# A lone half block as the sixteenth single block, row numbers read ahead, and turnings and the last shared batch in another order

## What is computed

```python
x = L0_attn_x                                  # 8 x 256 tokens, 256 features
x = x + attention(layernorm(x))                # 16 heads, running sums of phi(k) * v
h = layernorm(x)
logits = h @ router_w                          # 8 experts
top_logits, top_indices = top_k(logits, 2)
scores = softmax(top_logits)
routed: for each token and each of its 2 experts e
    g, u = split(h @ w1[e]); y = (silu(g) * u) @ w2[e]; out += score * y     # 256 -> 2*512 -> 256
shared = (silu(h @ w_gate) * (h @ w_up)) @ w_down                            # 256 -> 1024 -> 256
out = x + routed + shared
```

## Time and profile before

| what | value |
|---|---|
| median of 3 runs | 350.57 us (350.32 to 350.61) |
| the profiled execution, its own time | 352.41 us |
| its span, first to last instruction | 350.8 us |
| TensorE busy | 336.1 us, 96% of the span |
| VectorE / ScalarE / GpSimd busy | 235.2 / 203.8 / 199.8 us |
| mean granted TensorE clock | 0.997 |

### The profile page before, as it was taken

One profiled execution on the slowest core, in us unless ns is written; L12 is line 12 of the kernel. 1 busy time (PEld: TensorE's weight loads), 2 busy tenths in 40 slices (PEclk: granted clock), 3 DMA queues, 4 the chain that ended last, 5 costly groups with the idle time before them and its releaser, 6 DMA issues.

```text
span 350.8 us, 9452 instructions
## 1 busy us (share of the span) xinstructions
PE 336.1 (96%) x3082; PEld 276.6 (79%) x3082; DVE 235.2 (67%) x584; ACT 203.8 (58%) x369; POOL 199.8 (57%) x299
## 2 busy tenths in 40 slices
PE   8999999999999999999999999999899999999991
PEld 7779878888888888988988455656468888888880
DVE  4999989899889887878788565555433344443440
ACT  2779959797887987746536354364353434443340
POOL 4776567786875868565656443453443453336443
PEclk9999999999999999999999999999999999999998
DMA  7992152564965556735774345667674176544434
GB/s 190 390 348 49 30 127 48 131 150 160 198 198 91 150 164 144 214 102 132 256 260 110 96 68 74 101 88 86 97 103 68 22 95 73 62 63 61 62 44 48
DMA packets 65774, 43.43 MB, mean 124 GB/s; under 512 B 49600, under 2 KB 60864, under 8 KB 65344
## 3 DMA queue, kind: packets, MB, share of 16 engines
q1 hardware_dynamic: 51664, 32.32, 36.0%
q0 software_dynamic: 9392, 10.44, 18.8%
q10 hardware_dynamic: 4672, 0.07, 1.0%
HBM read 19.09 MB, written 12.97 MB: 91 GB/s over the span
## 4 chain that ended last, share of the span: by engine, by line
PE 69%; DVE 14%; issue 5%; DMA 5%; ACT 3%; SPq 2%; POOL 0%; POOLq 0%; DVEq 0%
PE bU L247 13%; PE bG L247 13%; PE bU L1153 6%; PE bD L1030 5%; PE bG L1153 5%; PE bV L1218 4%; PE bQ L1218 3%; DVE ab L1694 3%; PE bQ L1174 3%; PE bV L1174 3%; PE bQ L247 2%; PE bV L247 2%; DMA xT<-rows 2%; PE bK L247 2%; DMA wd<-in_w_att 2%
## 5 line engine op out<-in xcount | busy, mean ns | idle before, releaser
L1694 DVE SCALAR_TENSOR_TENSOR ab<-bU,sg 128x512 f32<-128x512 f32 x64 | 44.2, 690 | 65.3 <-PE bU L247 32.1
L825 POOL DMA_INDIRECT out_y<-xs,dst_row x32 | 50.0, 1563 | 57.7 <-DVE dst_row L2037 28.1
L1343 ACT ACTIVATE sg<-bG 128x512 f32<-128x512 f32 x64 | 38.0, 593 | 45.4 <-PE bG L247 26.1
L598 POOL DMA_INDIRECT x_rows<-rows,slot_u x32 | 42.2, 1318 | 15.3 <-issue 14.2
L1508 ACT ACTIVATE ws_h<-ab 128x512 f16<-128x512 f32 x36 | 22.7, 629 | 47.0 <-DVE ab L1694 43.0
L2022 DVE TENSOR_TENSOR ws_h<-ab,ws_h 128x512 f16<-128x512 f32 x36 | 25.0, 694 | 20.8 <-ACT ws_h L1508 19.7
L1350 ACT ACTIVATE ah<-ab 128x512 f16<-128x512 f32 x32 | 20.1, 629 | 28.9 <-DVE ab L1694 28.8
L247 PE MATMUL bG<-work,we 128*128 128x256 f16 x240 | 29.5, 273 | 0.0
L247 PE MATMUL bU<-work,we 128*128 128x256 f16 x240 | 29.5, 273 | 0.0
L247 PEld LDWEIGHTS bG<-work,we 128*128 x240 | 23.4, 98 | 2.9 <-issue 0.2
L247 PEld LDWEIGHTS bU<-work,we 128*128 x240 | 23.4, 98 | 2.7
(11 more groups left out here) (358 smaller groups left out, 874.0 us busy)
## 6 DMA issues: line engine op xcount, KB each, us to landing
stage<-in_w_expert SPq DMA_DIRECT2D x24, 512.0 KB
we<-in_w_shared SPq DMA_DIRECT2D x3, 1024.0 KB, 11.5
out_y<-xs SPq DMA_DIRECT2D x8, 256.0 KB
xs<-bo POOLq DMA_DIRECT2D x7, 256.0 KB, 4.3
xs<-in_x SPq DMA_DIRECT2D x1, 1280.0 KB, 17.5
x_rows<-we SPq DMA_DIRECT2D x9, 134.0 KB
xs<-in_x SPq DMA_DIRECT2D x3, 256.0 KB, 4.4
work<-x_rows SPq DMA_TRANSPOSE x40
```

What stands on the lines that cost most here:

```text
L598: pool.indirect_dma_start(xrows, bass.IndirectOffsetOnAxis(ap=slot_u[q][:, k, t:t + 1], axis=0), rows2[q][:, t, :].bitcast(U16), None).the ...
L825: pool.indirect_dma_start(out_rows, bass.IndirectOffsetOnAxis(ap=dst_row[:, b:b + 1], axis=0), ya[b % NY], None, bounds_check=NT * P - 1, ...
L1343: act.activation(sg[q][:], src[:], ACT.Silu, scale=1.0 / WS).then_inc(S["sg_done"], 1)
L1694: dve.scalar_tensor_tensor(out=ab[q][:], in0=src[:], scalar=1.0 / WS, in1=sg[q][:], op0=ALU.mult, op1=ALU.mult).then_inc(S["a_done"], 1)
```

## The change

1. Block 15 (`LONE`) becomes a half block of 64 rows. Gate and up are done in two column tiles: the same 64 rows are stationary in both, tile 0 makes columns 0 to 255 and tile 1 columns 256 to 511, so 6 pairs of matmuls of 256 columns. Its down is 12 pairs of 128 columns. The activations are 128 x 256 instead of 128 x 512, two matmuls turn them. Its weights come from the lent copies: four copies at the end of block 13 on VectorE and two at the end of block 15. Its meta data is loaded in two halves on ScalarE, its output goes out as half rows of 128 columns with one more small index operation on VectorE. GpSimd makes six more constants, four of them in the last group, `slot_constants(4)`.
2. SyncE reads 12 row numbers into registers of their own (upper halves of the four mixed blocks, blocks 4 to 11) after it has saved the last batch and before `turn_low(0)`; `load_rows` for these reads none.
3. `turn_high(b-1)` stands behind both up-projections of block b instead of between them, for b = 1, 2, the mixed blocks and 15.
4. In the last shared batch on VectorE `shared_out(6)` and the two spread copies move back, behind `swiglu` and `act_lo` of chunks 2 and 3; `expert_lo` of part 22 comes before them.

```diff
+    LONE = NS - 1
+    HALVED = MIXED + [LONE]
-    N_CONST = 41
+    N_CONST = 47
...
+        def width(b):
+            return FE // 2 if b == LONE else FE
...
+            ahead = [(b, 1) for b in MIXED] + [(b, 0) for b in range(NX, NX + 8)]
+            ahead_reg = {s: sp.alloc_register(f"row_of{s[0]}_{s[1]}") for s in ahead}
...
-                sp.reg_load(row_reg[t], blk_row[slot:slot + 1, :])
+                if (b, t) not in ahead:
+                    sp.reg_load(reg, blk_row[slot:slot + 1, :])
...
             save(B - 1)
+            for s in ahead:
+                slot = slot_of(*s)
+                sp.reg_load(ahead_reg[s], blk_row[slot:slot + 1, :])
...
+                elif b == LONE:
+                    pool.nop(nofuse=True)
+                    pool.indirect_dma_start(half_rows, bass.IndirectOffsetOnAxis(ap=dst_row[:, NBLK:NBLK + 1], axis=0),
+                                            ya[b % NY][:, 0:D // 2], None, bounds_check=2 * NT * P - 1, oob_is_err=False,
+                                            compute_op=ALU.add).then_inc(S[f"scattered{b % 2}"], 16)
...
+            def turned_late(b):
+                return b in HALVED or b in (1, 2)
...
+            def lone_up(half):
+                dst, done, free = ((bG, "g_ps", "sg_done"), (bU, "u_ps", "a_done"))[half]
+                if half == 0:
+                    pe.wait_ge(*rows_in(LONE))
+                    pe.wait_ge(S["lent"], 6 * NPAIR + 4)
+                pe.wait_ge(S[free], NP * B + LONE)
+                x2, n = xg[LONE % NX], FE // 2
+                for s, (hi, lo) in enumerate(((0, 0), (1, 0), (0, 1))):
+                    w = lent_up[:, lo, :].rearrange("p (k h n) -> p k h n", k=KC, h=2)
+                    for k in range(KC):
+                        for t in range(2):
+                            ins = pe.matmul(dst[t * HALF:(t + 1) * HALF, 0:n], x2[:, hi * KC + k, 0:HALF], w[:, k, half, t * n:(t + 1) * n],
+                                            start=s == 0 and k == 0, stop=s == 2 and k == KC - 1, skip_group_check=True)
...
+            def lone_down():
...
+                    for c in range(FC):
+                        at = c // 2 * HALF
+                        for t in range(2):
+                            ins = pe.matmul(dst[t * HALF:(t + 1) * HALF, 0:m], a[:, c % 2, at:at + HALF], lent_down[:, c, lo, t * m:(t + 1) * m],
...
             for b in range(NS):
-                expert_up(b, 0)
-                if b >= 1:
+                if b == LONE:
+                    lone_up(0)
+                    lone_up(1)
+                else:
+                    expert_up(b, 0)
+                    if b >= 1 and not turned_late(b):
+                        turn_high(b - 1)
+                    expert_up(b, 1)
+                if turned_late(b):
                     turn_high(b - 1)
-                expert_up(b, 1)
...
-                if b <= NS + 1:
+                if b == NS:
                     expert_down(b - 2)
+                elif b == NS + 1:
+                    lone_down()
...
-                parts = 2 if b in MIXED else 1
+                parts = 2 if b in HALVED else 1
...
             expert_lo(part_of_step(B, 4))
-            shared_out(B - 2)
             swiglu(n + 2, 0)
+            expert_lo(part_of_step(B, 5))
+            act_lo(j, 2)
+            swiglu(n + 3, 1, bV)
+            act_lo(j, 3)
             dve.wait_ge(S["spread_ps"], 1)
...
-            expert_lo(part_of_step(B, 5))
-            swiglu(n + 3, 1, bV)
-            act_lo(j, 2)
-            act_lo(j, 3)
             expert_lo(part_of_step(B, 6))
+            shared_out(B - 2)
...
+                if b == MIXED[-1]:
+                    for k in range(4):
+                        lend_weights(NPAIR, k)
+                if b == LONE:
+                    for k in range(4, 6):
+                        lend_weights(NPAIR, k)
```

More of the change, by code:

```diff
@@ L319, in meta_in @@
                 return S[f"first_meta{b}"], 16
-            return S[f"meta_in{b % NX}"], sum(32 if n in MIXED else 16 for n in range(b % NX + NX, b + 1, NX))
+            return S[f"meta_in{b % NX}"], sum(32 if n in HALVED else 16 for n in range(b % NX + NX, b + 1, NX))
         def paired(b):
@@ L338, in slot_of @@
         def slot_of(b, t):
-            return b if t == 0 else HALF + MIXED.index(b)
+            return b if t == 0 else HALF + HALVED.index(b)
+        def width(b):
+            return FE // 2 if b == LONE else FE
         def mixed_of(a):
@@ L607, in const @@
                     pool.wait_ge(S["slot_const"], n_const[0])
-            evens, list_pos, here = half_f[:, 1:NPAIR + 1], slot_w[:, 1, 0:1], slot_w[:, 0, 1:NPAIR + 1]
+            odds, list_pos, here, lone = half_f[:, 1:NPAIR + 1], slot_w[:, 1, 0:1], slot_w[:, 0, 1:NPAIR + 1], slot_w[:, 0, 0:1]
             def slot_constants(k):
@@ L643, in slot_constants @@
                     const(pool.tensor_scalar(pick_block[:], iota_f[:, 0:NBLK], place_at[:], None, ALU.is_equal))
-                    const(pool.tensor_scalar(slot_w[:, 2, 0:1], upper[:, 1:2], 1.0, None, ALU.mult), wait=True)
+                    const(pool.tensor_scalar(lone, place_at[:], float(LONE), None, ALU.is_equal))
+                    const(pool.tensor_scalar(slot_w[:, 2, 0:1], place_at[:], float(LONE), upper[:, 1:2], ALU.is_lt, ALU.mult), wait=True)
                 else:
@@ L650, in slot_constants @@
                     const(pool.tensor_scalar(mix_past[:], mix_at[:], float(NPB), list_pos, ALU.add, ALU.is_lt))
-                    const(pool.tensor_tensor(at_slot[:, 0:1], at_slot[:, 4:5], at_slot[:, 5:6], ALU.add), wait=True)
+                    const(pool.tensor_scalar(late[:], lone, 3.0, None, ALU.mult))
+                    const(pool.tensor_scalar(at_slot[:, 1:2], lone, -float(LONE + NPB), None, ALU.mult))
+                    const(pool.tensor_scalar(at_slot[:, 0:1], at_slot[:, 4:5], at_slot[:, 5:6], lone, ALU.add, ALU.add), wait=True)
+                    const(pool.tensor_tensor(list_pos, list_pos, at_slot[:, 1:2], ALU.add))
+                    const(pool.tensor_scalar(mix_past[:], mix_past[:], late[:], None, ALU.subtract), wait=True)
                     const(pool.tensor_tensor(slot_w[:, 1, 1:NPAIR + 1], mix_thr[:], mix_past[:], ALU.subtract))
@@ L1131, in turn_high @@
                     pe.wait_ge(S["ath_done"], b)
-                for c in range(FC):
+                for c in range(width(b) // P):
                     ins = pe.matmul(bK[:, c * P:(c + 1) * P], ar_h[b % NA][:, c * P:(c + 1) * P], ident16[:], start=True, stop=True)
@@ L1338, in silu @@
             def silu(n, q, src=bG):
+                m = width(n - NP * B)
                 act.wait_ge(S["g_ps"], n + 1)
@@ L2047, in lend_weights @@
             def lend_weights(q, k):
-                b = MIXED[q]
                 if q == 0 and k == 0:
```

63 lines of the change are left out of this document (43 added, 20 removed).

## The result

The changed kernel takes 348.56 us (median of six), the kernel before it in the same session 350.59 (350.32 to 350.92): a ratio of 0.9936, 95% interval 0.9918 to 0.9954. Five of the six took 347.5 to 349.3 (median 348.36), and one, at 352.98 and a granted clock of 0.988 where the others have 0.992 to 0.996, is in a slower state and counts in the median of 348.56 but not in the ratio. It is faster by 2.0 us, by the ratio 2.2. The forecast of 345.9 was 2.7 too low, and the range of 345.0 to 348.2 missed it by 0.4 (0.2 with the median of the five). The profiled execution took 349.26 (span 347.6). Repeated in another session the ratio was 0.9947 (0.9927 to 0.9967).

The account below looks back on a forecast made before the run. TensorE, busy 96% of the span, was taken to bound the kernel. 1.0 + 0.88 + 1.62 + 1.57 - 0.4 = 4.7 off the profiled 352.41 gives 347.7; less 1.84, a median of 345.9, range 345.0 to 348.2.

Parts of the forecast that it names:

- The lone block: Block 15: gate through down(13) 1.08 less, block 15's turning 0.11 and its down 0.43 less; term 1.62.
- rival B: Blocks 15 and 16: VectorE copies and ScalarE meta loads hold, 128-column pairs cost like 256: 347.7; chance 0.12.
- The 0.4 for thin covers: Around the lone block: 0.4 taken off for extra copies, meta loads and constants with little slack (ends 0 and 1.5).
- The mixed blocks: Late turnings leave two of four changes between full and 64-wide matmuls per mixed block: term 4 x 0.22 = 0.88.
- the term of 1.57: Block 11's down: reads ahead free SyncE, its transpose leaves on time and the wait goes: 1.57 gained.
- rival A: Block 11: the plain runs don't have its wait, so the 1.57 is nothing: 347.4; chance 0.22.
- turn_low(0) ... leaves at 198.7: Before down(0): twelve reads delay the transpose to 198.7, landing 202.1; 0.4 late, inside block 3's 0.5 wait, costing nothing.
- rival C: SyncE: twelve register loads hold turn_low(0), landing 10.2 late at their most: 355.6, slower; chance of slower 0.05.
- GpSimd's index chain ... feels 0.5: End of block 1: spread copies 3.5 later delay the chain and small matmul 0.5, which block 1's end has room for.
- The late constants on GpSimd ... fall into 1.06 idle: GpSimd before its last row writes: four constants of 0.2 to 0.3 fit into 1.06 idle.
- point 4's gain: Last shared batch: the wait for VectorE's low part goes, gain 0.46; together with blocks 1 and 2's turnings, 1.0.
- Rival D: Whole change: waits move instead of going, only 0.9 of the lone block's 1.6 counts: 349.7; chance 0.07.

Follow-up runs that it names:

- e8: Lone block alone (point 1, with block 14's late turning) on the kernel before, points 2, 3 and 4 undone: 349.62 us, 0.9977.
- e4: Kernel before, unchanged, profiled once more: profiled time 350.05 us.
- e7: Kernel before with the twelve reads ahead alone (point 2): 350.18 us, 0.9999.
- e11: Changed kernel, unchanged, profiled and timed again (also called "after again"): 348.82 us, 0.9947.
- e1: Changed kernel with SyncE's twelve reads moved in front of the saves of the last two shared batches: 347.79 us, 0.9927.
- e14: e13 with only six reads ahead of block 0's low part and the other six behind block 7's rows: 346.77 us, 0.9895.
- e13: Changed kernel, spread copies back, ScalarE's high part of chunk 3 before its last weight part, lone-block constants one step earlier; SyncE as changed: 348.70 us, 0.9947.
- e5: e1 with VectorE's two spread copies moved back to their earlier place: 348.09 us, 0.9935.
- e3: Kernel before with points 2, 3 (mixed blocks, 1 and 2) and 4, without the lone block: 349.79 us, 0.9982.
- e16: e14 plus block 2's expert load ahead of block 0's turning and VectorE's sixth-matrix low part behind the product of (7,3): 346.85 us, 0.9894.
- e17: Kernel before with VectorE's low part of the sixth matrix part just ahead of the spread copies: 351.03 us, one time.

## Why the prediction missed

**Right.** *The lone block:* block 15 to the pairs takes 3.19 instead of 4.34, 1.15 less against 1.08 predicted. From the pairs to the end the three profiles of after, after again and e8 take 89.2 to 89.3 and the two of before 89.6 to 89.8: about 0.45 less against 0.54. The pairs of 128 columns ran at half the time of those of 256 (0.68 for twelve), so that part of rival B is out, and so is its other part: no wait of blocks 15 or 16 shows. The 0.4 for thin covers wasn't spent where I put it. *The mixed blocks:* 47.08 to 46.26 from block 4 to 15, 0.82 against 0.88. *The turnings of blocks 1 and 2* wait no more.

**Wrong, the term of 1.57.** The prediction's step "Without the register loads it has 2 us more and the transpose goes out once the low part is ready" costed a wait that the plain runs don't have: e4 lacks it, and e7, which has the reads ahead alone, gains nothing (0.9999). This was rival A, and by itself it gives 347.4. The profile of before had said so: its own time was 1.84 above the median. The sum took the wait as a gain and then subtracted those 1.84 as well as if they were something else.

**Wrong, "turn_low(0) ... leaves at 198.7. Landings take 3.4 in the median: 202.1. ... nothing".** The twelve reads took 4.4 us from the first start to the transpose. Most stood 0.29 apart, as I had used; but the first two and the fifth took 0.71, 0.51 and 0.44 instead of 0.27, which my median left out. The transpose left at 199.3 and landed 4.5 later, at 203.8, where I had 202.1: 0.6 of these 1.7 are the reads', 1.1 the landing's, which took 4.5 and not the 3.4 of the earlier trace rows. Down(0) waited 1.3, and the gate of block 3 was 1.4 later than in the kernel before (0.8 in e11), not 1.0 earlier. e1, which only moves the reads, gives back 0.9 to 1.5 at block 3; e14 against e13 gives 0.54. The sign of rival C's mechanism was right; its price was 2 us and not 10, and more of that was the landing than the reads.

**Wrong, "GpSimd's index chain ... feels 0.5 ...; block 1's end has that room".** Block 1's end had 1.7 us of room before: the chain ended at 29.4 and the spread matmul came at 31.06 (all behind the logit gap). In the changed kernel TensorE comes there earlier and the chain ends at 30.6, and the gate of block 2 goes from 31.09 to 31.28. The copies weren't the cause (e5, e13). The chain was late by the lone block's constants (0.6) and by two waits for VectorE (0.4 and 0.5); a third, at the casts between them, was 0.2 shorter than before. Point 4 moved VectorE's instructions against GpSimd's, which I had costed only by who needs the results.

**Wrong, "The late constants on GpSimd ... fall into 1.06 idle".** The idle time in the earlier trace rows ended with `slot_u`, but the constants are also awaited: VectorE's first instruction of the plan waited 0.45 for them, and block 0 came 0.6 late (e8 against before). It took most of point 4's gain, which without it is 0.70 (e3), more than my 0.46; so block 0 starts only 0.14 earlier than before.

**The sum again**, from the profiles behind the logit gap, against the kernel before run again: 0.8 to 1.4 lost at block 4 where 1.0 was to be gained; 0.8 gained in the mixed blocks, 1.15 and some 0.5 by the lone block. That leaves 1.1 to 1.6 in the profiles, and the medians say 1.9 to 2.2 (0.9947 and 0.9936 of 350.5). The difference of some 0.7 stays open; the landing of the first low part differs from execution to execution (4.5 and 4.2 us after its issue in two profiles, 3.5 and 3.3 in e3 and e13 with the same order on SyncE), and quicker ones would give it, which is argued and not shown. Rival D, waits that move instead of going, describes the opening.

## What to carry to other kernels

A wait that one profile shows is a gain only if the plain runs have it. Where the profiled time lies above the median by the size of that wait, take a second profile before counting it. Work taken from the middle of a full queue and put at its head is paid for by the first instruction behind it: read as many numbers ahead as are needed soon, and the rest later (e14 against e13, where all twelve stand at the head: 0.9895 against 0.9947). And when VectorE's order changes, lay GpSimd's small instructions beside it: an instruction of 0.2 us can take 0.7.

## What the hardware showed that I had not expected

A gather on GpSimd takes 0.96 or 1.96 us by whether a VectorE instruction with two SBUF operands starts just after or just before it (e16, e17). Most of twelve reads of a register in a row took 0.27 us and stood 0.29 apart, but three of them took 0.71, 0.51 and 0.44; TensorE's read ahead of block 2 took 0.71 to 0.81 beside the saves' transfers in four of four runs and 0.30 to 0.31 in all others. The same transpose of a low part landed 2.4 us after its issue in both profiles of the kernel before, 4.2 to 4.5 in those of the changed one and 3.3 in e13. The lone block's down, two column tiles with streams of only 128 columns, ran at 0.056 us a pair behind the first, as fast per column as streams of 256.
